# Reading tile numbers into registers one tile at a time instead of eight or sixteen at once, in a graph network kernel

## What is computed

```python
def spmm(h):                                   # twice in layer 0
    msg = h[src] * edge_w[:, None]
    agg = jax.ops.segment_sum(msg, dst, num_segments=N)
    return agg + self_w[:, None] * h
h = relu(batchnorm(spmm(x @ W1 + b1)))
x = layernorm(x + spmm(h @ W2 + b2))
# layer 1: attention over edges, 8 heads; row = src, col = dst
scores = einsum('ehd,ehd->eh', q[row], k[col]) / 4 + edge_emb @ eb_w.T + eb_b
exp_scores = exp(scores - segment_max(scores, row)[row])
attn = exp_scores / (segment_sum(exp_scores, row)[row] + 1e-10)
out = segment_sum(attn[..., None] * v[col], row)
x = layernorm(x + (out.reshape(n, 128) @ out_w.T + out_b))
```

## Time and profile before

| | |
|---|---|
| time, median of 3 runs | 9340.34 us (9325.51 to 9343.74) |
| the profiled execution | 9325.89 us, its span 9324.3 us |
| busy, PE / PEld / DVE / ACT / POOL | 73 / 61 / 67 / 36 / 64 % of the span |
| mean granted TensorE clock | 0.79 of full speed |

### The profile page before, as it was taken

How to read it: one execution, slowest core, us unless ns; L and a number is a source line. 1 busy time by engine, 2 the same in 40 slices (tenths; PEclk the granted TensorE clock), 3 DMA queues, 4 the chain that set the end, 5 groups by cost and what they waited for, 6 DMA issues and landing times. The chain is left out here.

```text
span 9324.3 us, 229377 instructions
## 1 busy us (share of the span) xinstructions
PE 6847.9 (73%) x40334; PEld 5733.4 (61%) x40335; DVE 6225.0 (67%) x23634; ACT 3314.6 (36%) x10654; POOL 5973.0 (64%) x6648
## 2 busy tenths in 40 slices
PE   7789999999868888888884656666666577735774
PEld 5578888888747777776773444444444466625663
DVE  8755555555547777777776655555555688897777
ACT  7533333333324444444441100000000233316884
POOL 4467776666656666666667577777777455526665
PEclk9876666666668888888885888888888899978997
DMA  1043333333342211111112333333333544414553
GB/s 45 8 113 104 105 104 104 102 102 102 89 124 53 52 51 51 51 50 50 48 49 62 110 113 113 113 113 113 113 113 113 140 126 125 126 51 131 151 153 93
DMA packets 1057790, 868.52 MB, mean 93 GB/s; under 512 B 214825, under 2 KB 950425, under 8 KB 1057737
## 3 DMA queue, kind: packets, MB, share of 16 engines
q0 software_dynamic: 179664, 437.87, 15.4%
q1 hardware_dynamic: 643032, 319.49, 13.1%
q10 hardware_dynamic: 235040, 110.58, 4.2%
HBM read 578.04 MB, written 287.84 MB: 93 GB/s over the span
## 5 line engine op out<-in xcount | busy, mean ns | idle before, releaser
L1420 POOL DMA_INDIRECT spmm_rows<-h_table,spmm_index_ring x3136 | 2968.3, 947 | 1472.4 <-issue 886.2
L1491 PE MATMUL bank<-spmm_rows,spmm_hot 128*128 x6660 | 1951.2, 395 | 117.8 <-SPq L1397 71.1
L1765 POOL DMA_INDIRECT kv_sorted<-expand_payload,expand_where_ring x1568 | 1519.1, 969 | 500.6 <-issue 418.4
L1465 DVE TENSOR_TENSOR region_ab<-region_ab,bank 128x128 f32 x3330 | 956.1, 287 | 1213.9 <-PE bank L1491 1165.9
L1786 PE MATMUL bank<-region_ab,expand_hot_t 128*128 x3336 | 1107.5, 490 | 773.4 <-DVE expand_hot_t L1802 773.1
L1491 PEld LDWEIGHTS bank<-spmm_rows,spmm_hot 128*128 128x128 f32 x6660 | 1421.9, 265 | 214.0 <-issue 184.3
L1818 DVE SCALAR_TENSOR_TENSOR expand_payload<-expand_payload,region_c,bank 128x256 f32 x1668 | 801.5, 481 | 893.7 <-SPq L1730 406.2
L1786 PEld LDWEIGHTS bank<-region_ab,expand_hot_t 128*128 128x128 f32 x3336 | 770.8, 242 | 975.2 <-issue 849.0
L1449 DVE TENSOR_SCALAR spmm_hot<-iota_bf,lo_slots 128x128 f32<-128x128 bf16 x3334 | 1001.3, 300 | 20.0 <-issue 18.7
L1946 POOL TENSOR_TENSOR score_qk<-score_q_sb,score_k_rows 128x512 f32<-128x512 f32 x420 | 532.3, 1267 | 477.4 <-ACT score_q_sb L1895 464.2
L456 ACT ACTIVATE spmm_beside_sign<-iota_half,region_c 128x128 bf16<-128x128 bf16 x1568 | 521.8, 392 | 828.8 <-DVE spmm_beside_bias_sb L545 681.0
(11 more groups left out here) (350 smaller groups left out, 13957.6 us busy)
## 6 DMA issues: line engine op xcount, KB each, us to landing
score_k_rows<-kv_sorted SPq DMA_DIRECT2D x420, 288.0 KB
mix_mixed<-kv_sorted SPq DMA_DIRECT2D x420, 256.0 KB
spmm_beside_attr_sb<-in_edge_attr_dram ACTq DMA_DIRECT2D x390, 256.0 KB
spmm_rows<-h_table,spmm_index_ring POOLq DMA_INDIRECT x3136
kv_sorted<-expand_payload,expand_where_ring POOLq DMA_INDIRECT x1568
kv_sorted<-spmm_beside_blank SPq DMA_DIRECT2D x1, 15232.0 KB
kv_sorted<-spmm_beside_blank SPq DMA_DIRECT2D x98, 136.0 KB
h_table<-region_ab SPq DMA_DIRECT2D x28, 448.0 KB, 3.0
```

The costliest lines, as they stand in the source:

```text
L1420: nc.gpsimd.indirect_dma_start(rows[:, h * HALF + k, :], None, table, bass.IndirectOffsetOnAxis(ap=index_ring[:, h, k:k + 1], axis=0)).the ...
L1465: nc.vector.tensor_tensor(here, here, sum_bank[k % 2][:, 0:D], ALU.add).then_inc(added, 1)
L1491: nc.tensor.matmul(sum_bank[k % 2][:, 0:D], hot[:, k % HOTS, :], tile_of(rows, place[k % HALF]), start=True, stop=True).then_inc(summed, 1)
L1765: nc.gpsimd.indirect_dma_start(kv_sorted, bass.IndirectOffsetOnAxis(ap=where_ring[:, h, k:k + 1], axis=0), payload[:, h * HALF + k, 0:ROW] ...
```

## The change

Three places are edited, besides one move. In the sparse products DVE reads one node number, and PE one place and one count, at the head of every tile. In mix DVE reads the two places of a pair ahead of that pair. In score the load of four node numbers stays as it is but is issued ahead of the spreading of keys instead of behind it.

```diff
# sparse_product, DVE
-                        for h in range(-(-tiles // HALF)):
-                            node = loaded(mybir.EngineType.DVE, node_d[0:1, bass.ds(i * TURN + h * HALF, HALF)], HALF, NT - 1, CLAMPED)
-                            for k in range(h * HALF, min(tiles, (h + 1) * HALF)):
-                                t = i * TURN + k
...
+                        for k in range(tiles):
+                            t = i * TURN + k
+                            node, = loaded(mybir.EngineType.DVE, node_d[0:1, bass.ds(t, 1)], 1, NT - 1, CLAMPED)
...
+                            here = tile_of(nodes, node)
# sparse_product, PE
-                            if k % HALF == 0:
-                                some = bass.ds(t, HALF)
-                                place = loaded(mybir.EngineType.PE, window_place[:, some], HALF, TURN, WINDOW_SLOT)
-                                until = loaded(mybir.EngineType.PE, until_window[:, some], HALF, E_COLS, CLAMPED, least=1)
+                            place, = loaded(mybir.EngineType.PE, window_place[:, bass.ds(t, 1)], 1, TURN, WINDOW_SLOT)
+                            until, = loaded(mybir.EngineType.PE, until_window[:, bass.ds(t, 1)], 1, E_COLS, CLAMPED, least=1)
# score, PE
+                        node = loaded(mybir.EngineType.PE, node_at[0:1, bass.ds(i * TURN + j * GROUP, GROUP)], GROUP, NT - 1, CLAMPED)
                         if not (static_turn(i, S_TURNS - 1) and j == GROUPS - 1):
                             spread_keys(g + 1, (j + 1) % 2, i * TURN + (j + 1) * GROUP)
-                        node = loaded(mybir.EngineType.PE, node_at[0:1, bass.ds(i * TURN + j * GROUP, GROUP)], GROUP, NT - 1, CLAMPED)
# mix, DVE
-                    _, place = nc.values_load_multi_w_load_instructions(
-                        sum_places[:, bass.ds(i * TURN, TURN)], engines=[mybir.EngineType.DVE],
-                        min_val=0, max_val=NT, skip_runtime_bounds_check_because=CLAMPED)
...
+                            place = loaded(mybir.EngineType.DVE, sum_places[:, bass.ds(i * TURN + k * 2, 2)], 2, NT, CLAMPED)
```

More of the change, by code:

```diff
@@ L1452, in turn @@
                     def turn(i, edges=True, tiles=TURN):
-                        for h in range(-(-tiles // HALF)):
-                            node = loaded(mybir.EngineType.DVE, node_d[0:1, bass.ds(i * TURN + h * HALF, HALF)], HALF, NT - 1, CLAMPED)
-                            for k in range(h * HALF, min(tiles, (h + 1) * HALF)):
-                                t = i * TURN + k
[L1457 to L1465, removed]
+                        for k in range(tiles):
+                            t = i * TURN + k
+                            node, = loaded(mybir.EngineType.DVE, node_d[0:1, bass.ds(t, 1)], 1, NT - 1, CLAMPED)
+                            if edges:
+                                work.vector_step(dve, i, k)
+                            one_hot(t + 2, k + 2)
+                            if edges:
+                                work.vector_end_step(dve, i, k)
+                            dve.wait_ge(summed, t + 1)
+                            need(dve, added, t)
+                            here = tile_of(nodes, node)
+                            nc.vector.tensor_tensor(here, here, sum_bank[k % 2][:, 0:D], ALU.add).then_inc(added, 1)
                     work.vector_start(dve)
@@ L1489, in turn @@
                             need(pe, added, t - 1)
-                            pe.wait_ge(arrived, until[k % HALF])
-                            nc.tensor.matmul(sum_bank[k % 2][:, 0:D], hot[:, k % HOTS, :], tile_of(rows, place[k % HALF]),
+                            pe.wait_ge(arrived, until)
+                            nc.tensor.matmul(sum_bank[k % 2][:, 0:D], hot[:, k % HOTS, :], tile_of(rows, place),
                                              start=True, stop=True).then_inc(summed, 1)
@@ L2237, in turn @@
                                 need(dve, added, i * TURN + k * 2 + stream - 1)
-                                here = tile_of(sums, place[k * 2 + stream])
+                                here = tile_of(sums, place[stream])
                                 v.tensor_tensor(here, here, bank[k % RING][:, stream * W:(stream + 1) * W], ALU.add).then_inc(added, 1)
```

## The result

The changed kernel takes 11,129.1 us (median of four runs, 11,124.9 to 11,131.8) against 9,341.3; the ratio is 1.192, 95% interval 1.190 to 1.194. The forecast was 10,570 us with a range to 11,100: the direction was right and so was the price of a small load; the size was 560 us short, outside the range, nearly all of it in spmm2, where a step of the reasoning failed.

A forecast was written before the change was run, and what follows sets the result against it. No engine was full; queues and waits mattered, and PE's queue would bound the sparse products. 9325.9 + 408 + 490 + 375 - 40 = 10,559 us, put at 10,570 for the median; range 10,050 to 11,100.

The forecast's parts named there:

- spmm2: Second sparse product: PE's queue with its small loads needs 13.7 us for eight tiles against 11.2, +490 us (+410 to +800).
- The price of a small load: Register loads on PE and DVE: one register taken as 0.27 us, two as 0.52, from the repeated rows.
- The rival in which small loads lie on the line of the large ones: All small loads: 0.142 us for one register, 0.206 for two, so about 9,490 us in all; chance 0.08.
- the one with the single occurrences: Small loads cost what was seen once, 0.5 us on PE, 0.77 for two on DVE: about 12,190 us; chance 0.05.
- The rule of equal cost for each register: All loads: a register costs the same in any load, 74 ns, giving 9,230 us; chance 0.03.
- spmm1: First sparse product: PE's queue becomes the bound, 12.3 us for eight tiles against 10.2, +408 us.
- the sum of the queue: PE in the sparse products: issue, sixteen small loads and branch added for eight tiles, 12.3 us in spmm1, 13.7 in spmm2.
- the ring: Sparse products, from the experiments: PE's sum, DVE's add, load, one-hots, PE's matmuls and loads, next sum; once per tile pair.
- Mix: DVE's queue in mix: eight loads of two replace one of sixteen per turn, 10.4 us against 6.84, +375 us.
- Score: Load of four moved ahead of the key spreading, products come up to 0.3 us sooner: -40 us (+60 to -90).
- The rival on the other side: PE in spmm2: its queue runs far enough ahead to hide the loads, about 9,020 us in all; chance 0.03.

The follow-up runs named there:

- the fillers: Six matmuls a tile that compute nothing used, added to the changed kernel: in spmm2 alone 10,774 us, in both sparse products 10,703 us.

## Where the prediction went wrong

**The price of a small load** was read rightly from rows far away. One register on PE cost 0.302 us where 0.27 was taken from SyncE, with a range of 0.25 to 0.30, at whose end it lies; two on DVE cost 0.527 for 0.52. The rival in which small loads lie on the line of the large ones would have had 0.142 and 0.206, and the one with the single occurrences 0.496 and 0.767: both are out. The rule of equal cost for each register is out too: 302 ns for one, 74 each in a group of eight. The Trainium skill (Runtime: NRT & Kernel Launch, Instruction fetch mechanics) gives about 200 ns for a register even in bulk, on a page that describes such loads as coming from HBM. Here they come from SBUF: one register took 302 ns, two 264 each, four 83 each and eight 74 each, so the figure doesn't hold for groups. The Trainium skill's floor of about 600 ns for a `tensor_load` (DMA: Bandwidth & Descriptors, Latency and other measured facts) does not hold here: 302, 342 and 527 ns are all below it.

**spmm1** was put at 12.3 us for eight tiles and took 12.6 (2444 us over 1551 tiles). The price of the load adds 0.5 to my sum and makes 12.8. The sum is thus right to 2%, but that is in part luck. It put the clock and DVE's load at nothing, and each had a share: 12.2 with the clock back up (the fillers' own issue in it), and 12.3 with DVE's load moved. With the right price the sum of the queue is above the measured time, so that a little of it is covered after all.

**spmm2** is the step that failed, in two sentences of the prediction: "DVE in spmm2 is busy 1665 us in 2200 ...; with 0.43 more it needs 11.9 for eight, below 13.7", and "PE's clock matters less than before, since matmuls are no longer the bound". The first compared how full two queues are and left out that they wait for each other in a ring. The second took the clock as a matter of a full engine. The clock fell from 0.83 to 0.50 over the stretch, and that lengthened PE's part of the ring. What the runs showed in place of 13.7 us for eight tiles: the changed kernel took 16.2. With DVE's load off the ring it took 15.0, with the clock back at 0.99 14.4, and with both 14.4 (3179, 2930, 2823 and 2815 us). The price of the loads adds 0.5 to the forecast sum (16 x 0.032 us) and makes 14.2. So the sum of the queue was nearly right for a kernel without the ring at the half clock, and what it left out is some 1.8 to 2.0 us for eight tiles. The 1.8 can't be split into a part of the clock and a part of DVE's load, since the two act on the same way around. The 11.2 that was subtracted should have been 11.35, which makes the forecast growth 461 us and the miss 30 us larger than the table says. The upper end of this term, +800, was made from waits that are not covered; it was also too low, since no end of it held a change of the clock.

**Mix** was right: +345 for +375, and alone as in the whole, though PE's clock was 0.76 in the changed kernel and 0.92 before.

**Score** was called -40 and is 0. That a load is hidden at one place says nothing while the next instructions come later by the same amount; the profile before gave no step at which the queue would issue less.

**The rival on the other side**, that PE's queue runs far enough ahead to hide the loads, needed less than 0.3 us for a load with its setup; it costs 0.46. The run with loads of four answers it too, since even there nothing was gained.

Shown are the price, that the place of DVE's load decides over 248 us in spmm2, PE's waits for the one-hots behind it, and the clock's part. Only argued are which limit lies under the ring, and why PE's clock fell. It stood at 0.50 in every run with PE's loads in every tile and no fillers, and at 0.57 or more in spmm1 and 0.79 or more in spmm2 in the runs that left PE's loads in groups. No run here separates the spacing of matmuls from their number. The 189 us that DVE's load alone cost in spmm1 are not taken apart.

## What to carry to other kernels

Price a register load by how many registers it brings: here groups of four are cheap and single ones dear, so read in groups, even unused ones, and put the group behind work already handed out instead of splitting it. When two queues wait for each other, add up the way around, not how full each is. When a change thins out PE's matmuls, ask what the granted clock will do to every step that waits for a matmul, also where PE is far from full.

## What the runs showed of the hardware that was not expected

- A TENSOR_LOAD of two registers takes 528 ns, one of four 342 (DVE, same place, same tensor); one 302, four 330, eight 590 on PE.
- The granted clock of PE fell from 0.83 to 0.50 over a stretch of 3.2 ms in which the profile still calls PE busy for 88% of the time; six short matmuls a tile brought it to 0.99 and made a kernel with 9,990 more matmuls 355 us faster. The Trainium skill (TensorE: Matmul & The Clock Gate, What's actually happening) has the clock follow how busy PE has been recently. By the number of matmuls the runs agree in direction: spmm2 has 6.0 for each us at a clock of 0.83 before, 4.2 at 0.50 after, and 8.1 at 0.99 with the fillers. By the share that the profile calls busy they don't: 82, 88 and 79%.
